# A gated cross-attention and expert layer on one core: the key mask as one row, another order of weight transposes, and other places of the fill-in matmuls

## The reference

```
h = x + tanh(g_x) * xattn(layernorm(x), ctx, ctx, mask)
out = h + tanh(g_f) * moe(layernorm(h))

xattn: Q = q @ wq.T + bq; K = ctx @ wk.T + bk; V = ctx @ wv.T + bv     (16 heads of 16)
       scores = Q K^T / 4; -inf where key > query, and where the key is masked
       probs = softmax(scores), or 1/77 if every score is infinite
       return (probs V) @ wo.T + bo
moe:   logits = h @ Wr + br; gate = max softmax; one expert of 8 per token
       y = gate * (relu(ln(h) @ W1[e] + b1[e]) @ W2[e] + b2[e])      (256 -> 1024 -> 256)
```

## Time and profile before

| | us |
|---|---|
| median of 3 runs | 287.1 |
| lowest and highest | 286.43 and 289.65 |
| the profiled execution | 286.55 |
| its span in the profile | 284.7 |
| TensorE busy in the span | 273.6 (96%) |
| DVE, ACT, POOL busy | 208.6, 165.7, 137.5 |

### The profile page before, as it was taken

One profiled execution on the slowest core, in us unless ns is written; L12 is line 12 of the kernel. 1 busy time (PEld: TensorE's weight loads), 2 busy tenths in 40 slices (PEclk: granted clock), 3 DMA queues, 4 the chain that ended last, 5 costly groups with the idle time before them and its releaser, 6 DMA issues.

```text
span 284.7 us, 7387 instructions
## 1 busy us (share of the span) xinstructions
PE 273.6 (96%) x2382; PEld 238.5 (84%) x2382; DVE 208.6 (73%) x682; ACT 165.7 (58%) x444; POOL 137.5 (48%) x259
## 2 busy tenths in 40 slices
PE   5999999999999999999999999999999999999993
PEld 2768898889898888998779889999879789988992
DVE  3678489999999999988887986795554745534554
ACT  3333467777777777767567574786527545443551
POOL 3325245577777777544688622644302342222331
PEclk9799999999999999999999999999999999999999
DMA  6999995011101555455133221422112102210211
GB/s 188 311 307 372 374 383 190 39 40 39 40 37 41 186 187 185 151 187 185 69 96 102 94 79 59 128 62 63 58 41 59 54 22 81 75 58 21 60 56 59
DMA packets 19834, 34.44 MB, mean 121 GB/s; under 512 B 2534, under 2 KB 14628, under 8 KB 19785
## 3 DMA queue, kind: packets, MB, share of 16 engines
q1 hardware_dynamic: 15369, 21.26, 22.7%
q0 software_dynamic: 4128, 12.49, 13.6%
q10 hardware_dynamic: 288, 0.09, 0.1%
HBM read 27.47 MB, written 6.75 MB: 120 GB/s over the span
## 4 chain that ended last, share of the span: by engine, by line
PE 82%; DVE 8%; issue 3%; ACT 2%; DMA 2%; POOL 1%; ACTq 0%; DVEq 0%; POOLq 0%
PE pS L1825 19%; PE pB L1599 11%; PE pB L1895 10%; PE pT L1509 6%; PE pB L1619 6%; PE pB L1900 5%; PE pA L1509 4%; PE pS L1553 3%; PE pA L1532 3%; PE pT L1532 2%; DMA W2s<-in_L_xattn_bk_dram 2%; PE pT L1629 2%; DVE hA L1272 1%; PE pT L1850 1%; PE pT L1870 1%
## 5 line engine op out<-in xcount | busy, mean ns | idle before, releaser
L1825 PE MATMUL pS<-znf,W1c 128*128 128x128 f32 x576 | 71.3, 277 | 0.1
L1825 PEld LDWEIGHTS pS<-znf,W1c 128*128 128x128 f32 x576 | 67.1, 192 | 3.4 <-issue 2.8
L452 POOL DMA_INDIRECT out_dram<-yo,idxs x17 | 17.3, 1020 | 71.7 <-DVE yo L1303 67.2
L1599 PEld LDWEIGHTS pB<-VB,PT 128*128 128x128 f32 (+1 forms) x320 | 38.1, 192 | 3.0 <-issue 3.0
L1599 PE MATMUL pB<-VB,PT 128*128 128x51 f32 (+1 forms) x320 | 39.5, 272 | 0.8 <-DVE xs L928 0.3
L739 ACT ACTIVATE hA<-pS,b1s 128x128 f32<-128x128 f32 x72 | 20.5, 367 | 33.8 <-PE pS L1825 31.0
L1895 PE MATMUL pB<-W2p,hT 128*128 128x512 f32 x136 | 38.9, 408 | 0.2 <-DVE ticks L1312 0.2
L600 ACT ACTIVATE Pb<-Pb 128x616 f32<-128x616 f32 x32 | 22.9, 717 | 19.0 <-DVE Pb L906 19.0
L1272 DVE TENSOR_SCALAR hA<-pS,b1s 128x128 f32<-128x128 f32 x72 | 20.2, 343 | 18.6 <-PE pS L1825 18.6
L750 ACT ACTIVATE hT<-hA 128x512 fp32r<-128x512 f32 x36 | 23.2, 645 | 14.3 <-DVE hA L1272 14.2
L435 POOL DMA_INDIRECT zin<-rows_dram,idxg x21 | 23.2, 1105 | 11.5 <-issue 5.3
(11 more groups left out here) (278 smaller groups left out, 533.6 us busy)
## 6 DMA issues: line engine op xcount, KB each, us to landing
W1s<-in_L_ffn_W_dram SPq DMA_DIRECT2D x8, 1024.0 KB, 10.7
W2s<-in_L_ffn_W_dram SPq DMA_DIRECT2D x8, 1024.0 KB, 11.3
rows_dram<-pay POOLq DMA_DIRECT2D x16, 260.0 KB, 3.0
xs<-in_x_dram SPq DMA_DIRECT2D x3, 512.0 KB, 6.1
W2s<-in_sel_dram SPq DMA_DIRECT2D x1, 385.0 KB
zin<-rows_dram,idxg POOLq DMA_INDIRECT x21, 3.7
out_dram<-yo,idxs POOLq DMA_INDIRECT x17, 2.5
W1s<-in_L_xattn_wk_dram SPq DMA_DIRECT2D x1, 256.0 KB, 4.7
```

The lines of the kernel that those rows point to most:

```text
L1599: t = e.matmul(pB[:, 17 * h0:17 * h0 + 51], PT[i % 2][0:n, c, :], VB[0:n, b, c, :], start=(c == 0), stop=(c == NC - 1), skip_group_check=True)
L1825: t = e.matmul(pS[:, 2 * (s % 2) + n, 128 * c:128 * c + 128], W1c[k][n][:, 128 * c:128 * c + 128], znf[s % 2][:, 128 * k:128 * k + 128], s ...
```

## The change

- The mask is loaded into one partition. DVE computes on that row, with eight instructions, the valid keys, their complement, the counts, and the other numbers that were computed on 128 partitions. Two matmuls with a row of ones spread them over the partitions (`v_all` in bank pB; `m_all` and `n_all` in a bank of pS), and two more give the mask's columns (`v_col`). They are put in front of wk's transposes. DVE reads the results from PSUM; `CV` is made from `ctxT` in SBUF.
- wq's transposes go in front of those of bq and bk; one of the single fill-ins goes. wv's transposes go to bank T1, the wait for their copy moves from `scores(0)` to V, and ACT copies them before tanh.
- The three groups of `WARM[1]` fill-ins, behind wv's transposes, behind V and in front of tile 0's first `transpose_P`, go.
- ACT's first query copy goes behind `KT`'s second half; tanh and `copy_XX(1)` go in front of the first exp. DVE's `stats1(1)` goes in front of `key_blocks(1)`. V's bias matmuls go in front of the others.

```diff
@@ -163,6 +163,7 @@
...
         bvr = stage("W1", D, 1)
         one_row = stage("W1", 128, 1)
+        row = PT1[0:1, 0:3, :].rearrange("p c n -> p (c n)")
         scr = stage("W1", 320)
         selv = stage("W2", NC * 128, LK)
@@ -172,7 +173,6 @@
...
         vnat = stage("W2", B * H * 17, LK).rearrange("p (b h w) -> p b h w", b=B, w=17)
         brow = stage("W2", 128, 4)
-        KI = stage("W2", B * LK).rearrange("p (b k) -> p b k", b=B)
         upper = stage("W1", 128)
         bst = W2s[:, 5 * 2048:5 * 2048 + F + D]
...
@@ -217,6 +217,11 @@
...
         nb, nall, aall, nbc, rn, oma = (vm[:, 0:2], vm[:, 2:3], vm[:, 3:4], vm[:, 4:6], vm[:, 6:8], vm[:, 8:9])
         csum, cmean = vm[:, 10:14], vm[:, 14:18]
+        valid_row, masked_row, n_row = row[:, 0:B * LK], row[:, B * LK:2 * B * LK], row[:, 2 * B * LK:2 * B * LK + 9]
+        v_all = pB[:, 0:B * LK]
+        m_all = pS[:, 1, 0:B * LK].rearrange("p (b k) -> p b k", b=B)
+        n_all = pS[:, 1, B * LK:9 + B * LK]
+        v_col = pS[0:LK, 2, 480:482]
         mhalf, mone = powers[:, 0:1], powers[:, 1:2]
         bank = {"A": pA[:, :], "B": pB[:, :], "S0": pS[:, 0, :], "S1": pS[:, 2, :], "T0": pT[:, 0, :],
@@ -642,7 +647,7 @@
...
 
             e.dma_start(ident, consts[:, 0:128]).then_inc(d["id"], 16)
-            e.dma_start(maskr[:, :], mask.rearrange("b k -> (b k)").partition_broadcast(128)).then_inc(d["mr"], 16)
+            e.dma_start(maskr[0:1, :], mask.rearrange("(o b) k -> o (b k)", o=1)).then_inc(d["mr"], 16)
             e.wait_ge(g["pe_ctxT"], 1)
             e.activation(ctxT, pctx, ACT.Copy).then_inc(g["act_ctxT"], 1)
@@ -651,10 +656,13 @@
...
             e.wait_ge(g["dve_bcol"], 1)
             e.activation(KT[:, 0, :], pS[:, 0, LK:2 * LK], ACT.Identity, bias=bkc[:, 0:1]).then_inc(g["act_KT"], 1)
-            query(0)
             e.wait_ge(g["dve_Kbd"], 2)
             e.activation(KT[:, 1, :], pS[:, 3, LK:2 * LK], ACT.Identity, bias=bkc[:, 1:2]).then_inc(g["act_KT"], 1)
-            copy_wT(3, "wv", "S1")
+            query(0)
+            copy_wT(3, "wv", "T1")
+            e.wait_ge(d["gg"], 32)
+            e.activation(tg[:, :], gx[:, :], ACT.Tanh).then_inc(g["act_tg"], 1)
+            copy_XX(1)
             a_steps = Count()
             for n in range(NT):
@@ -663,10 +671,7 @@
...
                 exp(n, 0)
                 if n == 0:
-                    copy_XX(1)
                     exp(0, 1)
-                    e.wait_ge(d["gg"], 32)
-                    e.activation(tg[:, :], gx[:, :], ACT.Tanh).then_inc(g["act_tg"], 1)
                 if n:
                     copy_PT(n - 1, 1)
@@ -1123,62 +1128,63 @@
...
 
             e.memset(onesb[:, :], 1.0).then_inc(g["dve_ones"], 1)
-            e.memset(one_row, 1.0).then_inc(g["dve_one_row"], 1)
+            e.memset(one_row, 1.0).then_inc(g["dve_ones"], 1)
             e.memset(vm[:, 18:19], 1.0 / D).then_inc(g["dve_ones"], 1)
             e.memset(taken[:, E:9], 0.0).then_inc(g["dve_ones"], 1)
             e.memset(capped[:, 0:1], 0.0).then_inc(g["dve_ones"], 1)
             e.memset(bst, 0.0).then_inc(g["dve_bst"], 1)
+            def on_row(t):
+                t.then_inc(g["dve_row"], 1)
+
             e.wait_ge(d["mr"], 16)
-            e.tensor_scalar(v2, maskr[:, :], -1.0, 1.0, ALU.mult, ALU.add).then_inc(g["dve_valid"], 1)
-            e.wait_ge(g["dve_valid"], 1)
-            e.tensor_reduce(nb, valid[:, :, :], AX.X, ALU.add).then_inc(g["dve_own"], 1)
-            t_nb = own.up()
+            on_row(e.tensor_scalar(valid_row, maskr[0:1, :], -1.0, 1.0, ALU.mult, ALU.add))
+            e.wait_ge(g["dve_row"], 1)
+            on_row(e.tensor_reduce(n_row[:, 0:2], valid_row.rearrange("p (b k) -> p b k", b=B), AX.X, ALU.add))
+            on_row(e.tensor_scalar(masked_row, valid_row, -1.0, 1.0, ALU.mult, ALU.add))
+            e.wait_ge(g["dve_row"], 2)
+            on_row(e.tensor_scalar(n_row[:, 4:6], n_row[:, 0:2], 1.0, None, ALU.max))
+            on_row(e.tensor_tensor(n_row[:, 2:3], n_row[:, 0:1], n_row[:, 1:2], ALU.add))
+            e.wait_ge(g["dve_row"], 4)
+            on_row(e.reciprocal(n_row[:, 6:8], n_row[:, 4:6]))
+            e.wait_ge(g["dve_row"], 5)
+            on_row(e.tensor_scalar(n_row[:, 3:4], n_row[:, 2:3], 0.0, None, ALU.is_equal))
+            e.wait_ge(g["dve_row"], 7)
+            on_row(e.tensor_scalar(n_row[:, 8:9], n_row[:, 3:4], -NEG, NEG, ALU.mult, ALU.add))
+            e.wait_ge(g["pe_all"], 1)
             e.wait_ge(g["act_ctxT"], 1)
-            e.tensor_tensor(CV.rearrange("p k b n -> p k (b n)"), pctx,
-                            v2.unsqueeze(1).broadcast_to([128, 2, B * LK]), ALU.mult).then_inc(g["dve_CV"], 1)
-            e.wait_ge(g["dve_own"], t_nb)
-            e.tensor_scalar(nbc, nb, 1.0, None, ALU.max).then_inc(g["dve_own"], 1)
-            t_nbc = own.up()
-            stats1(0)
+            e.tensor_tensor(CV.rearrange("p k b n -> p k (b n)"), ctxT,
+                            v_all.unsqueeze(1).broadcast_to([128, 2, B * LK]), ALU.mult).then_inc(g["dve_CV"], 1)
+            e.wait_ge(g["pe_all"], 2)
+            e.tensor_copy(vm[:, 0:9], n_all).then_inc(g["dve_own"], 1)
+            t_n = own.up()
             e.wait_ge(g["dve_CV"], 1)
             e.tensor_reduce(csum.rearrange("p (k b) -> p k b", k=2), CV, AX.X, ALU.add).then_inc(g["dve_own"], 1)
-            own.up()
-            e.wait_ge(g["dve_own"], t_nbc)
-            e.reciprocal(rn, nbc).then_inc(g["dve_own"], 1)
-            t_rn = own.up()
-            e.tensor_scalar(KI, valid[:, :, :], -1.0, 1.0, ALU.mult, ALU.add).then_inc(g["dve_own"], 1)
-            own.up()
-            e.wait_ge(g["dve_own"], t_rn)
+            t_sum = own.up()
+            stats1(0)
+            e.wait_ge(g["dve_own"], max(t_n, t_sum))
             e.tensor_tensor(cmean.rearrange("p (k b) -> p k b", k=2), csum.rearrange("p (k b) -> p k b", k=2),
                             rn.unsqueeze(1).broadcast_to([128, 2, B]), ALU.mult).then_inc(g["dve_own"], 1)
             t_mean = own.up()
-            e.tensor_tensor(nall, nb[:, 0:1], nb[:, 1:2], ALU.add).then_inc(g["dve_own"], 1)
-            t_all = own.up()
             e.wait_ge(g["dve_own"], t_mean)
             for k in range(2):
                 for b in range(B):
-                    e.scalar_tensor_tensor(out=CV[:, k, b, :], in0=KI[:, b, :],
+                    e.scalar_tensor_tensor(out=CV[:, k, b, :], in0=m_all[:, b, :],
                                            scalar=cmean[:, 2 * k + b:2 * k + b + 1], in1=CV[:, k, b, :],
                                            op0=ALU.mult, op1=ALU.add).then_inc(g["dve_ck"], 1)
             normed1(0)
-            e.wait_ge(g["dve_own"], t_all)
-            e.tensor_scalar(aall, nall, 0.0, None, ALU.is_equal).then_inc(g["dve_own"], 1)
-            t_a = own.up()
+            e.tensor_copy(v2, v_all).then_inc(g["dve_own"], 1)
+            own.up()
+            e.wait_ge(g["pe_vcol"], 2)
             e.wait_ge(g["pe_bq"], 1)
+            e.tensor_scalar(vcol[0:LK, :], v_col, aall[0:LK, :], None, ALU.add).then_inc(g["dve_vcol"], 1)
             e.tensor_copy(bcol[:, 0:4], pS[:, 2, 0:4]).then_inc(g["dve_bcol"], 1)
-            e.wait_ge(g["pe_vcol"], 1)
-            e.wait_ge(g["dve_own"], t_a)
-            e.tensor_scalar(vcol[0:LK, :], pB[0:LK, 32:96].rearrange("p (b n) -> p b n", b=B)[:, :, 0], aall[0:LK, :],
-                            None, ALU.add).then_inc(g["dve_vcol"], 1)
-            e.tensor_scalar(oma, aall, -NEG, NEG, ALU.mult, ALU.add).then_inc(g["dve_own"], 1)
-            t_oma = own.up()
             e.wait_ge(d["cst"], 16)
             e.wait_ge(g["dve_bcol"], 1)
             key_blocks(0)
+            stats1(1)
             key_blocks(1)
-            e.wait_ge(g["dve_own"], t_oma)
+            e.wait_ge(g["dve_own"], own.n)
             mask_bias(0)
-            stats1(1)
             normed1(1)
             t_max = {}
@@ -1545,7 +1551,6 @@
...
                         e.wait_ge(g["pool_id"], 1)
                         e.wait_ge(g["act_KT"], 2)
-                        e.wait_ge(g["act_wT"], 3)
                     e.wait_ge(g["dve_bias0"], b + 1)
                 for m in range(2):
@@ -1660,16 +1665,20 @@
...
                     t = transpose(pA[:, 160 * k + LK * b:160 * k + LK * b + LK], ctxs[0:LK, b, 128 * k:128 * k + 128])
             t.then_inc(g["pe_ctxT"], 1)
+            e.wait_ge(g["dve_ones"], 2)
+            e.wait_ge(g["dve_row"], 2)
+            e.matmul(v_all, one_row, valid_row, start=True, stop=True).then_inc(g["pe_all"], 1)
+            e.wait_ge(g["dve_row"], 8)
+            e.matmul(pS[:, 1, 0:9 + B * LK], one_row, row[:, B * LK:2 * B * LK + 9], start=True, stop=True).then_inc(
+                g["pe_all"], 1)
+            for b in range(B):
+                e.matmul(v_col[:, b:b + 1], valid_row[:, LK * b:LK * b + LK], one_row[:, 0:1], start=True,
+                         stop=True).then_inc(g["pe_vcol"], 1)
             weight("wk", "T0")
```

(28 more changed lines are left out.)

## The result

| | before | after |
|---|---|---|
| median, 20 executions each | 287.82 us | 285.5 us |
| lowest and highest | 286.33 and 289.65 | 282.8 and 287.85 |
| ratio of the medians | | 0.9919 |
| ratio, with its interval | | 0.9899, 95% interval 0.9875 to 0.9923 |
| profiled execution, its span | 286.55, 284.7 | 287.61, 285.8 |

The change makes the kernel 2.3 us faster by the medians, 0.8%. The profiled execution of after is one of its slowest: 287.61 against a median of 285.5.

A forecast was written before the change was run, and what follows sets the result against it. TensorE, 82% of the chain, was taken to bound the kernel. Gains of 1.0, 0.9, 0.2, 0.75 and 0.65, less 0.2 at ln and some 0.7 to DVE, made 2.6: 284.5 from 287.1, range 282.9 to 286.6.

The forecast's parts named there:

- the signs that the prediction set itself: Wrong if wk starts after 6.5, another or longer half-clock stretch shows, or the attend's 2.6 is missing at the last tile.
- The likeliest case: Low clock stretch stays where it was, 2.6 us gained to the end: 284.5, own range 283.4 to 285.4, chance 50%.
- Step 1: Start, mask row: lands at 3.95, eight DVE results 1.4, matmuls 0.55 behind; wk's transposes start at 5.92, nothing lost.
- Step 2: TensorE before K: K starts at about 8.4 instead of 10.05, all at 1.2 GHz; gain 1.0 at its end.
- Step 3: K to scores(0): wait for wv's copy and fill-ins go, query copy late next; 1.0 more, 1.9 together.
- Steps 4 and 5: Scores(0) to first attend: V's order and removed fill-ins gain, DVE takes part back; attend at 24.1 instead of 26.74.
- I take it that the 2.6 reach the end.: After the first attend nothing is changed, so its 2.6 us gain is carried to the end of the kernel.
- Rival (b): A second low clock stretch where the fill-ins are gone costs TensorE 1.7 us: 286.2, chance 8%.
- Rival (a): Low stretch absent or where TensorE waits anyway; K starts at 8.1, 0.9 more gain: 283.6, chance 15%.
- (c): Mask row lands late, 4.8 to 6.3; at 5.65 K ends 0.5 later than now, 1.1 remains: 286.0, chance 12%.
- (e): Slower: mask row, in front of wk, lands after about 6.8; at 7.35 it is 0.6 slower, 287.7, chance 5%.

The follow-up runs named there:

- e1: The changed kernel run again for a second profile: median 285.39 us, ratio of the medians to before 0.9916.
- f1: The changed kernel run once more, giving its third profile: median 288.79 us where before took 290.53, ratio of the medians 0.9940.
- e8: The changed kernel with the mask loaded to 128 partitions as before, only the first used: median 289.25 us, ratio of the medians to before 0.9974.
- e3: The kernel of before without the nine fill-ins, nothing else changed: median 288.13 us, ratio of the medians to before 1.0011.
- e2: The changed kernel with its three removed groups of three fill-ins put back: median 286.39 us, ratio of the medians to before 0.9950.
- e6: The changed kernel with five fill-ins in TensorE's waits and two inside the 8-column matmuls: median 286.18 us, ratio of the medians to before 0.9868.
- f2: The changed kernel with seven fill-ins, in TensorE's waits and the 8-column matmuls, run again: median 286.39 us, ratio of the medians to before 0.9858.
- f4: The changed kernel with wk's transposes ahead of three of the four mask matmuls: median 289.24 us, ratio of the medians to before 0.9956.
- e5: The changed kernel with five fill-ins where TensorE waits, three between tile 0's probability transposes, two behind scores(2): median 287.63 us, ratio of the medians 0.9918.
- e7: The changed kernel without the four fill-ins between wk's transposes and K: median 288.75 us, ratio of the medians to before 0.9957.

## Why the prediction was right, and where it was off

Forecast were 2.6 us at the first attend and at the end: 284.5 from 287.1. Measured are 2.3, 285.5 from 287.82; of the 1.0 between the times, 0.7 is that the first three executions of before lay low.

The time came out as forecast, the mechanism in part: the row, its landing and DVE's chain are as forecast. But by the signs that the prediction set itself it fails: wk's transposes start at 6.69 in the first profile (the limit was 6.5), all three profiles of the changed kernel have another or a longer stretch of half speed, and the 2.6 at the attend is -0.5, 1.2 and 3.2 at the last tile. The likeliest case, one low stretch in its old place and none after it, is none of the three. That the median is near 2.3 is luck in so far as a start that is better than forecast in some executions and worse in others is set off against a second stretch that was not in the sum.

- **Step 1, the row.** Landing forecast at 3.95, between 3.95 and 7.35: measured 3.6 to 4.1. The identity's load, just ahead in the same queue, was the right row to take. The eight results took 1.20 (4.14 to 5.20 + 0.14) for 1.4; what stands behind the last of them, 0.79 at the full clock (5.18 to 5.97 in e1) for 0.55. wk's transposes were forecast at 5.92 and came at 5.97 in e1 and 5.74 in f1. In the first profile they came at 6.69: its four matmuls on the row ran at half speed and ended 1.35 behind the last result, past the bound of 1.0; the forecast had no half-speed start among its cases.
- **What step 1 missed.** I took 5.92 as the landing of wk, which the change can't alter. It can: 2.9 to 3.3 us to landing with the row, in nine profiles, against 4.3 to 5.5 with 128 partitions, in five. The mask's load holds the others up: e8 is the changed kernel with that load alone put back, and wk takes 4.3, bk 4.7 (3.5 to 3.8 with the row). It made no difference to the forecast only because the row's chain stood there anyway.
- **Step 2, K.** Forecast at 8.4 with the low stretch in its old place; in the profile that has it there, 9.19, and the gain at the end of K 0.6 instead of 1.0 (11.18 against 11.8). The term that was off is wq's transposes and the fill-ins: I had the transposes' 0.45 and 0.1 of the fill-ins at the full clock before the fall, but the clock fell at about 7.1, and the transposes took 0.82 and the three fill-ins 1.39, nearly all of it at half speed.
- **Step 3, scores(0).** Forecast 1.9 earlier, measured 1.55 in that profile; the step by itself, from K's end, is 0.9 for 1.0. Expected was that scores(0) waits for ACT's query copy. It is a tie: the copy ends at 12.74, and TensorE's own transposes of wv, which stand in front of scores(0), at 12.77; the chain names these in all three profiles.
- **Steps 4 and 5.** Forecast 0.7 from scores(0) to the attend, measured 0.70 (11.70 against 12.40). But the account of it was wrong. I credited 0.75 and 0.65 to the removed fill-ins and took 0.9 away for DVE. e3 shows that alone they are worth 0.2 in the kernel of before. The 0.5 from scores(0) to value_blocks stands in two rows of the first profile: V's evacuation starts 4.60 behind scores(0) for 4.75 (18.89 - 14.29, 19.09 - 14.34; V's own order), and `normed1(2)` then waits 0.47 for GpSimd for 0.81, since the scaling of bo, behind tanh, runs at 15.17 instead of 20.02 and is out of the way. That is a reading of the rows; no run moved tanh by itself. The sum came out since I had let DVE's chain decide; the names on its terms did not.
- **"I take it that the 2.6 reach the end."** They don't. Rival (b), a second low stretch of 1.7, was given 8% and was there in all three profiles of the changed kernel, where it cost 0.9 to 1.3. The fill-ins taken away are not what it hangs on, as I had put it, for e2's profile has it with all of them and e3's has none without them, one profile each. Its cause stays open. TensorE's being busy is not enough for the full clock: in the first profile it was busy for 8.27 of 8.27 us from 4.40 to 12.67, at half speed, and in f1 the same instructions in the same order ran at the full clock from 4.83 on. By the page's rule on transposes ("TensorE: Matmul & The Clock Gate", "Part 4: PE-mode transpose", of the Trainium skill) these don't count as busy in the same way. These two profiles neither bear it out nor speak against it: they hold the same transposes, and the work ahead of the second stretch has the 8-column matmuls too; no run here separates the two.
- **Rival (a)**, no low stretch before K, was given 15% and 3.5 us: it is f1's profile, with the attend at 22.74, 4.0 earlier than before's. The lowest times of the first comparison, 282.8 against 286.33, 3.5 apart, are what it would give. Of the nine profiles with the row's load, some of variants, five have no low stretch before K (e2, e6, f1, f2, f4), three ran the whole start at half speed (the first, e5, e7), and one, e1, is the case that the sum was made for, but for its second stretch.
- **Rivals (c) and (e)**, the late row: not the case, but e8 made it so, and found the slope as worked out: 1.6 later, 1.4 at the attend.

So the 2.3 stands between executions in different states of the clock: the best of the two kernels are 3.5 apart, the worst 1.8 (287.85 against 289.65).

## What to carry to other kernels

Fill-ins are worth removing only where the next thing is ready: look for who is late next, and change that engine's order with it; e3 took them out alone and gained nothing, e2 kept them beside the new order and was 1.0 slower than the whole. A broadcast load of many small rows costs its neighbours too: with one row instead, wk landed 1.0 to 2.6 us earlier, and the row itself 1.4 to 2.9 earlier than the 128 rows, and the row's earlier landing took 1.4 us off the start here (e8). And where a start stage hangs on TensorE, one profile is one state of its clock: read two or three of the same kernel before a difference of 1 us is explained.

## What the runs showed of the hardware

- A 19.2 KB load of 128 rows of 154 bytes held up a 256 KB load that was issued at the same time on another queue: landing after 4.3 to 5.5 us instead of 2.9 to 3.3.
- The column of the granted clock can be wrong before its first recorded change: 1.00 is shown, while four transposes take 1.04 us in the chain instead of 0.59. In all 14 profiles the first recorded change is a rise, at 3.7 to 12.7 us.
- Low stretches of 3.4 us each came at other places in each profile of one program (behind the start: at 33.1; at 7.1 and 31.0; at 28.7), and the start ran at half speed up to 12.67, 3.72 and 4.83. In the first of them TensorE was busy without a pause from 4.40 on and yet at half speed until 12.67.
- A low stretch of 3.4 us at 28 to 36 us cost 0.9 to 1.3 us of the tiles' time in the three profiles of the changed kernel, not 1.7, half its length.
- A matmul of 163 columns from one-partition operands took 0.54 in the chain at the full clock where it waited for its operand (e1), and 0.32 where it stood right behind the matmul before it (f1). V's bias matmul of 256 columns took 0.58.
